# Layer 3's end in another order: the first element's normalisation and feed-forward blocks between the second one's last steps, the last addition and store in two

## The reference

```python
def _fq(x, delta, zp, n_bits):
    xi = _round_ste(x / delta) + zp
    xq = jnp.clip(xi, 0.0, 2.0 ** n_bits - 1.0)
    return (xq - zp) * delta
def _attn(x, ctx, wq, wk, wv, wo, bo, dq, dk, dv, dw):
    ...
    sim = jnp.einsum('bhid,bhjd->bhij', _fq(q, dq, 128.0, 8), _fq(k, dk, 128.0, 8)) * SCALE
    attn = jax.nn.softmax(sim, axis=-1)
    out = jnp.einsum('bhij,bhjd->bhid', _fq(attn, dw, 0.0, 8), _fq(v, dv, 128.0, 8))
    return out.transpose(0, 2, 1, 3).reshape(b, n, D) @ wo + bo
h1 = _ln(x, ln1_g, ln1_b)
x = _attn(h1, h1, a1_wq, a1_wk, a1_wv, a1_wo, a1_bo, d_q1, d_k1, d_v1, d_w1) + x
h2 = _ln(x, ln2_g, ln2_b)
x = _attn(h2, context, a2_wq, a2_wk, a2_wv, a2_wo, a2_bo, d_q2, d_k2, d_v2, d_w2) + x
h3 = _ln(x, ln3_g, ln3_b)
hg = h3 @ ff_w1 + ff_b1
a, g = jnp.split(hg, 2, axis=-1)
x = a * jax.nn.gelu(g, approximate=False) @ ff_w2 + ff_b2 + x
```

## Time and profile before

| | |
|---|---|
| runs, us | 547.52, 543.25, 539.63 (median 543.25) |
| profiled execution, us | 540.42 |
| its span, first to last instruction, us | 538.5 |
| mean granted TensorE clock | 0.784 of full |
| busy: PE, DVE, ACT, POOL | 77%, 66%, 47%, 45% |
| hidden blocks and output products of the feed-forward, from the first record to the last | 511.4 to 535.0 us |

### The profile page before, as it was taken

The page is one execution under the profiler, slowest core; times in us unless marked ns, Lnnn a source line. Parts: engine busy times, 40 slices in busy tenths (PEclk is TensorE's granted clock), DMA queues, the critical chain, the costliest instruction groups (busy, mean ns, idle before and its releaser), DMA issues.

```text
span 538.5 us, 8140 instructions
## 1 busy us (share of the span) xinstructions
PE 412.6 (77%) x2775; PEld 206.4 (38%) x2775; DVE 354.9 (66%) x802; ACT 254.0 (47%) x513; POOL 241.6 (45%) x378
## 2 busy tenths in 40 slices
PE   6889678757788999998989772566665756778597
PEld 3546455424334344334243550222232223324536
DVE  2744754556999311447384469999989898778442
ACT  2314433324000666643426327899977783447431
POOL 4051224349000344533201315999978896336320
PEclk9868957978999999999699996555555555556699
DMA  9400000000000000000000002698876677113301
GB/s 262 156 1 1 4 1 1 0 0 1 2 0 1 1 1 2 1 1 1 0 1 2 1 2 39 132 144 140 162 131 117 117 123 153 27 34 67 71 0 40
DMA packets 88975, 26.10 MB, mean 48 GB/s; under 512 B 81061, under 2 KB 88167, under 8 KB 88935
## 3 DMA queue, kind: packets, MB, share of 16 engines
q1 hardware_dynamic: 88935, 25.58, 24.5%
HBM read 5.61 MB, written 0.52 MB: 11 GB/s over the span
## 4 chain that ended last, share of the span: by engine, by line
PE 43%; DVE 27%; POOL 18%; issue 5%; ACT 4%; DMA 1%; POOLq 0%; DVEq 0%; ACTq 0%
POOL k_stack L573 12%; DVE k_stack L2068 8%; PE ps L837 5%; PE ps L852 4%; PE ps L638 3%; POOL stats L564 3%; PE ps L739 3%; DVE stats L2148 3%; PE ps L749 2%; DVE xh L1639 2%; PE ps L915 2%; DVE st L1630 2%; PE ps L630 2%; POOL rstd L483 2%; PE ps L773 2%
## 5 line engine op out<-in xcount | busy, mean ns | idle before, releaser
L2148 DVE TENSOR_REDUCE stats<-ps 128x2 f32<-128x1024 f32 x64 | 77.6, 1213 | 2.4 <-PE ps L1293 2.0
L1595 ACT ACTIVATE e_buf<-ps,stats,sders 128x512 f32<-128x512 f32 x88 | 67.6, 773 | 18.4 <-POOL stats L564 18.4
L1313 PE MATMUL ps<-k_stack,q_stack 128*32 128x128 bf16 x512 | 38.3, 307 | 37.9 <-DVE k_stack L2161 37.9
L573 POOL TENSOR_SCALAR k_stack<-e_buf,stats 128x512 int16<-128x512 f32 x88 | 63.0, 728 | 2.1 <-DVE stats L2155 1.5
L1441 ACT ACTIVATE e_buf<-ps 128x1024 f32<-128x1024 f32 (+3 forms) x44 | 28.2, 710 | 58.5 <-PE ps L837 58.5
L481 POOL TENSOR_SCALAR rstd<-mv 128x4 f32<-128x4 f32 x18 | 4.4, 243 | 99.3 <-DVE mv L1633 99.3
L1313 PEld LDWEIGHTS ps<-k_stack,q_stack 128*32 128x32 bf16 x512 | 22.0, 129 | 68.8 <-DVE k_stack L2161 66.0
L430 POOL TENSOR_SCALAR_AFFINE_SELECT e_buf<-e_buf 128x256 f32<-128x256 f32 x44 | 17.8, 412 | 66.8 <-ACT e_buf L1441 66.2
L1293 PE MATMUL ps<-q_stack 32*128 32x512 bf16 x128 | 37.6, 588 | 12.4 <-ACT e_buf L1595 8.9
L2068 DVE TENSOR_REDUCE k_stack<-ps 128x4 f32<-128x1024 f32 (+3 forms) x32 | 44.9, 1483 | 2.6 <-PE ps L796 2.6
L837 PE MATMUL ps<-k_stack,q_stack 32*128 32x512 f32 (+3 forms) x256 | 34.7, 478 | 0.6 <-ACT e_buf L1441 0.4
(11 more groups left out here) (277 smaller groups left out, 892.9 us busy)
## 6 DMA issues: line engine op xcount, KB each, us to landing
wsq<-in_squares SPq DMA_DIRECT2D x3, 384.0 KB, 4.8
k_stack<-k_stack SPq DMA_TRANSPOSE x64, 3.1
spread<-in_spread SPq DMA_DIRECT2D x1, 896.0 KB, 6.7
x<-in_x SPq DMA_DIRECT2D x1, 512.0 KB, 4.4
l_w<-in_L_xattn_W_ff SPq DMA_DIRECT2D x2, 256.0 KB, 7.2
l_w<-in_L_xattn_fc_w SPq DMA_DIRECT2D x2, 256.0 KB, 7.8
l_w<-in_L_xattn_ff_w SPq DMA_DIRECT2D x1, 512.0 KB, 8.8
out<-x SPq DMA_DIRECT2D x2, 256.0 KB, 2.3
```

The source lines that it names most:

```text
L573: pool.tensor_scalar(t_rows[n % TURNING][:, j, :], e_ring[n % len(e_ring)][:, j, :], stats[:, 2, c:c + 1], 0.0, ALU.mult, ALU.add).then_in ...
L1313: mm = pe.matmul(ps[BAND * band:BAND * (band + 1), 7, qb * P:(qb + 1) * P], v_band[:, kb, b, V * band + v, :], t_keys[n % len(t_keys)][:, ...
L1595: act.activation(e_ring[n % len(e_ring)][:, j, :], ps[:, 2 * (n % 3) + j, :], ACT.Exp, bias=stats[:, 1, c:c + 1], scale=sders[:, 8:9], acc ...
L2148: dve.tensor_reduce(stats[:, 0, c:c + 2], ps[:, 2 * (n % 3):2 * (n % 3) + 2, :], AX, ALU.max, negate=True).then_inc(S("ints.nm"), 1)
```

## The change

Five edits, all in layer 3's end.

- PE: the first element's transposes and hidden block 0 come between the outputs of tiles 6 and 7. Block 1 comes after them, then the second element's projection, blocks 2 and 3, the first element's 16 products in two parts with the second element's transposes between, blocks 4 to 7, the second element's 16 products in two parts.
- DVE: `normal` of the first element comes before `keys` of tile 6. The gating of blocks 0 and 1 comes before the second element's addition and statistics, that of 2 and 3 before its `normal`, that of block 4 before the first element's last addition.
- ACT: `cross_out(1)` comes after the gelu of block 0.
- Banks: hidden blocks use 0 to 3, which the cross attention's scores had, so block 0 also waits for the last exponentials. The first element's transposes go to bank 6, the second's to 7.
- End: the second element's last 128 x 512 addition is two of 128 x 256, from banks 5 and 6, and its 256 KB store is two of 128 KB.

```diff
@@ -98,7 +98,7 @@
 PROJECTED_AT, ADDED_AT, RSTD_AT, TURNED_AT, QUERIES_AT, CROSS_AT = 40, 40, 44, 48, 50, PAIRS + 2
-HIDDEN = (2, 3, 6, 7)
+HIDDEN = (0, 1, 2, 3)
 PV_BEHIND = 2
@@ -350,7 +350,7 @@
         states = [(name, k) for names in (("L1.sa",), ("L1.ca",), ("L1.ff",), ("L2.sa",), ("L2.ca0", "L2.ca"),
-                                          ("L2.co", "L2.ff"), ("L3.sa",), ("L3.ca0", "L3.ca"), ("L3.co",), ("L3.ff",))
+                                          ("L2.co", "L2.ff"), ("L3.sa",), ("L3.ca0", "L3.ca"), ("L3.co", "L3.ff"))
                   for k in range(B) for name in names]
         def state(name, k):
@@ -418,8 +418,14 @@
                                            flat_rows[i % len(flat_rows)]).then_inc(done, 16)
             for k in range(B):
                 sp.wait_ge(S(final), count(*final.rsplit(".", 1)) + final_each * (k + 1))
-                sp.dma_start(half_rows(out_dram, k), half_rows(x, k)).then_inc(S("out.stored"), 16)
-            sp.wait_ge(S("out.stored"), 16 * B)
+                if stop >= 3 and k == B - 1:
+                    sp.dma_start(out_dram[:, T - 2:T, :], x[:, T - 2:T, :]).then_inc(S("out.stored"), 16)
+                else:
+                    sp.dma_start(half_rows(out_dram, k), half_rows(x, k)).then_inc(S("out.stored"), 16)
+                if stop >= 3 and k == 0:
+                    sp.wait_ge(S("L3.ff.part"), 1)
+                    sp.dma_start(out_dram[:, QB:T - 2, :], x[:, QB:T - 2, :]).then_inc(S("out.stored"), 16)
+            sp.wait_ge(S("out.stored"), 16 * (B + 1 if stop >= 3 else B))
@@ -749,22 +755,26 @@
                     pe.matmul(ps[:, banks[n % 4], :], tile(w1, c), half(xT, k), start=True, stop=True
                               ).then_inc(S("ff.h"), 1)
-            def gated_feed_forward(name, w1, w2):
-                pe.wait_ge(S("ffw.loaded"), 96)
-                for n in range(B * FC):
-                    k, c = divmod(n, FC)
-                    if n == FC - 1:
-                        turn_half(xh, "L3.ln3.xh", 1)
-                    if c == 0:
-                        pe.wait_ge(S("state.T"), state(name, k))
-                    if n >= 2:
-                        pe.wait_ge(S("ff.hid"), count(name, "hid") + n - 1)
-                    pe.matmul(ps[:, HIDDEN[2 * (n % 2)], :], tile(w1, c), half(xT, k), start=True, stop=True)
-                    pe.matmul(ps[:, HIDDEN[2 * (n % 2) + 1], :], tile(w1, FC + c), half(xT, k), start=True, stop=True
-                              ).then_inc(S("ff.h"), 1)
-                for k in range(B):
-                    out_rows(name, w2, k)
+            def gated(n):
+                k, c = divmod(n, FC)
+                if n == 0:
+                    pe.wait_ge(S("cross.exp"), T)
+                if c == 0:
+                    pe.wait_ge(S("state.T"), state("L3.ff", k))
+                if n >= 2:
+                    pe.wait_ge(S("ff.hid"), count("L3.ff", "hid") + n - 1)
+                pe.matmul(ps[:, HIDDEN[2 * (n % 2)], :], tile(l3_w1, c), half(xT, k), start=True, stop=True)
+                pe.matmul(ps[:, HIDDEN[2 * (n % 2) + 1], :], tile(l3_w1, FC + c), half(xT, k), start=True, stop=True
+                          ).then_inc(S("ff.h"), 1)
+            def gated_outputs(k, tiles, bank):
+                pe.wait_ge(S("ff.hid"), count("L3.ff", "hid") + FC * (k + 1))
+                for t in tiles:
+                    for c in range(FC):
+                        mm = pe.matmul(ps[:, bank, t * P:(t + 1) * P], tile(hid[:, c, :], k * QB + t), l3_w2[:, c, :],
+                                       start=(c == 0), stop=(c == FC - 1))
+                return mm
             def project_half(name, wo, k, bank):
                 pe.wait_ge(S("state.T"), state(name, k))
@@ -1106,6 +1116,10 @@
                             subtract(i - 1)
                         if i == QB - 1:
                             turn_half(xh, "L3.ln2.xh", 1, bank=7)
+                        if i == T + FLAT_VALUES_BEHIND - 1:
+                            turn_half(xh, "L3.ln3.xh", 0, bank=6)
+                            pe.wait_ge(S("ffw.loaded"), 96)
+                            gated(0)
                         if i >= FLAT_VALUES_BEHIND:
                             outputs(i - FLAT_VALUES_BEHIND)
                         if i < T:
@@ -1338,9 +1352,17 @@
                 subtract(1)
                 project_half("L3.ca0", W["L3_xattn_a1_wo"], 1, 7)
                 rest()
-                turn_half(xh, "L3.ln3.xh", 0)
+                gated(1)
                 project_half("L3.co", W["L3_xattn_a2_wo"], 1, 5)
-                gated_feed_forward("L3.ff", l3_w1, l3_w2)
+                gated(2)
+                gated(3)
+                gated_outputs(0, (0, 1), 4)
+                turn_half(xh, "L3.ln3.xh", 1, bank=7)
+                gated_outputs(0, (2, 3), 4).then_inc(S("add.o"), 1)
+                for n in range(FC, B * FC):
+                    gated(n)
+                gated_outputs(1, (0, 1), 5).then_inc(S("L3.ff.first"), 1)
+                gated_outputs(1, (2, 3), 6).then_inc(S("add.o"), 1)
@@ -1505,7 +1527,6 @@
                     if i == T:
                         cross_out(0)
                     rounded(i - FLAT_ROUND_BEHIND)
-                cross_out(1)
             def cross_out(b):
                 act.wait_ge(S("cross.pv"), QB * (b + 1))
@@ -1600,11 +1621,13 @@
                     if n == TURNED_AT:
                         state_out("L3.ca", col("L3_xattn_ln2_g"), col("L3_xattn_ln2_b"), [0], 6)
                 cross()
-                state_out("L3.ff", col("L3_xattn_ln3_g"), col("L3_xattn_ln3_b"), [0])
+                state_out("L3.ff", col("L3_xattn_ln3_g"), col("L3_xattn_ln3_b"), [0], 6)
                 for n in range(B * FC):
                     c = n % FC
-                    if n == FC - 2:
-                        state_out("L3.ff", col("L3_xattn_ln3_g"), col("L3_xattn_ln3_b"), [1])
+                    if n == 1:
+                        cross_out(1)
+                    if n == FC:
+                        state_out("L3.ff", col("L3_xattn_ln3_g"), col("L3_xattn_ln3_b"), [1], 7)
                     act.wait_ge(S("L3.ff.h"), count("L3.ff", "h") + n + 1)
                     if n >= 2:
                         act.wait_ge(S("L3.ff.hid"), count("L3.ff", "hid") + n - 1)
@@ -1912,9 +1935,10 @@
                             add_to_x("L3.co", 6, [0])
                             stats_of("L3.co.x", 0, range(QB))
                             means_of(0)
+                        if i == T + FLAT_SUMS_BEHIND:
+                            normal("L3.ln3", 0)
                         if i >= FLAT_KEYS_BEHIND:
                             keys(i - FLAT_KEYS_BEHIND)
-                    normal("L3.ln3", 0)
                 return maxima, recips, rest
@@ -2199,16 +2223,30 @@
                         cross_maxima(1)
                 cross_recips(0)
                 rest()
-                add_to_x("L3.co", 4, [1])
-                moments("L3.ln3", 1, "L3.co.x", 1)
-                for n in range(B * FC):
+                def gate(n):
                     k, c = divmod(n, FC)
-                    if n == 1:
-                        normal("L3.ln3", 1)
                     dve.wait_ge(S("L3.ff.gel"), n + 1)
                     dve.scalar_tensor_tensor(half(hid[:, c, :], k), ps[:, HIDDEN[2 * (n % 2)], :], col("L3_xattn_ff_b1", c),
                                              gel[:, n % 2, :], ALU.add, ALU.mult).then_inc(S("L3.ff.hid"), 1)
-                add_to_x("L3.ff", 4)
+                gate(0)
+                gate(1)
+                add_to_x("L3.co", 4, [1])
+                moments("L3.ln3", 1, "L3.co.x", 1)
+                gate(2)
+                gate(3)
+                normal("L3.ln3", 1)
+                gate(4)
+                add_to_x("L3.ff", 4, [0])
+                for n in range(FC + 1, B * FC):
+                    gate(n)
+                dve.wait_ge(S("L3.ff.first"), 1)
+                dve.wait_ge(S("L3.ff.biased"), count("L3.ff", "biased") + 2)
+                dve.tensor_tensor(x[:, QB:T - 2, :], ps[:, 5, 0:2 * P].rearrange("p (t d) -> p t d", d=D),
+                                  x[:, QB:T - 2, :], ALU.add).then_inc(S("L3.ff.part"), 1)
+                dve.wait_ge(S("L3.ff.o"), count("L3.ff", "o") + B)
+                dve.tensor_tensor(x[:, T - 2:T, :], ps[:, 6, 2 * P:4 * P].rearrange("p (t d) -> p t d", d=D),
+                                  x[:, T - 2:T, :], ALU.add).then_inc(S("L3.ff.x"), 1)
 def kernel(**inputs):
```

## The result

| | before | changed |
|---|---|---|
| median, us (20 runs each) | 539.46 (537.27 to 547.92) | 543.37 (541.53 to 549.44) |
| profiled execution, its span, us | 540.42, 538.5 | 541.80, 539.9 |
| mean granted TensorE clock | 0.784 | 0.779 |

The ratio of changed to before is 1.007, with a 95% interval from 1.0047 to 1.0093; timed again (first experiment) it is 1.0045, from 1.0014 to 1.0077. The change makes the kernel slower by some 2.4 to 3.8 us, which is far under 2% but clear of the noise.

What follows compares the result with a forecast made beforehand. PE's list was taken to bound this end: +0.45 - 1.25 - 0.6 + 0.85 + 1.65 + 1.65 = +2.75 us, with the tail 2.2 slower. That gave 542.6 or 545.4 by base, forecast 544.0, range 539.5 to 549.0.

Steps and rivals of the forecast that it cites:

- Step 1: The first element's `normal` ahead of tile 6's keys: PE's ten products of tile 6 start later, +0.45 us.
- Step 2: Transposes and block 0 ahead of tile 7's outputs: PE waits about 0.85 us ahead of block 0, before 1.25.
- Steps 3 and 4: Each element's 16 output products behind its own fourth block: PE waits for that block's gating, +1.65 us each.
- Step 5: The second element's `normal`, held back by gating on DVE, still precedes PE's need by 0.7 us: costs nothing.
- Step 6: The tail, last addition and store in halves: 0.3 us saved on each, -0.6 us.
- The sum: PE's terms give +2.75 us, its last product at 537.8; with the tail the kernel is 2.2 us slower.
- Rival 1: The clock falls in PE's new waits: +5 us, 549.0, or 3% slower if it stays down; chance 0.13.
- Rival 2: The clock rises by 508.6 instead of about 513.6: 2.4 us gained, undoing the 2.2, 541.6; chance 0.12.
- Rival 3: The second element's chain comes 2 us late: PE waits 1.3 us at its transposes, 545.3; chance 0.07.
- The level: Kernel time 544.0 us, the middle between 542.6 on the profiled execution's base and 545.4 on the runs' median.
- No change that can be measured: Whole kernel: 2.2 us slower is too little, as runs spread 1.5% and a measurement can tell about 2%.
- The range: Kernel time from 539.5 to 549.0 us, with chance 0.95 of staying within 2%.

Runs made afterwards that it cites:

- first experiment: The changed kernel run again with no edit, for a second trace; ratio to before 1.0045 (1.0014 to 1.0077).
- block 0 back: The changed kernel with hidden block 0 behind tile 7's outputs again; ratio to before 1.0013 (0.9982 to 1.0045).
- filled: The changed kernel with an unread 128 x 256 fp32 product in PE's wait ahead of block 0; ratio to before 0.9991 (0.9965 to 1.0018).
- products late: The changed kernel with all 16 output products of the first element behind block 7; ratio to before 1.005 (1.0013 to 1.0088).

## Why the prediction was right, step by step

- **The bound.** PE's list sets this end: in every kernel the last chain is PE with its waits, and each edit moved the end by what it did to them and to the clock.
- **Step 1** (tile 6's outputs 0.45 us later): from tile 5's to tile 6's outputs it is now 2.76 us (502.54 to 505.30) where it was 2.40: 0.36 us. But the term is too small here. Tile 6's outputs start 2.5 us after the mark in both traces of the changed kernel and 1.45 us before, so 1.05 us later (0.4 to 1.1 over the six traces with this order). The transposing DMA of tile 6 had landed about 2.1 us before its keys in the first trace and 1.1 in the second (issued at 499.26 and 500.83, 3.4 us to landing, keys at 504.75 and 505.28), so its keys no longer waited for it but for `normal`, and `normal` for POOL's root (1.24 us idle). The sum had taken both chains as they lay in before's one trace, where the root was ready 0.7 us ahead of the landing; the sign "0.45 us later after the landing" did not come.
- **Step 2** (0.85 us ahead of block 0): 0.96. Its length was right. What the sum left out is that this wait bears on the clock: without it (block 0 back, or filled) the clock rose 2.8 to 3.9 us sooner. In the sum it made no difference, since before had its 1.25 us in the same place and rose as late (10.0 us after the mark against 9.7 and 8.7).
- **Steps 3 and 4** (1.65 us each): 1.56 and 1.56. That both are the open gelu and gating is shown by the tile whose products covered 0.9 us of the second.
- **Step 5** (costs at nothing): the cover of 0.7 us held, `normal` done at 521.52 and needed at about 522.5. How close it is, the kernel with the products late shows: without them PE waits 2.59 us for it.
- **Step 6** (tail -0.6): -0.8. The addition saved 0.27, as taken, and the store 0.51, near the row's bound of 0.45 and not the 0.3 that I took. The Trainium skill (DMA: Bandwidth & Descriptors, Anatomy of one DMA) gives 0.3 for the bytes as well, an estimate from its rate, which was fitted to DMAs that GpSimd issues, while these are SP's; the median landing of 2.3 us for 256 KB and 1.8 for 128 KB says 0.5.
- **The sum** had +2.2 us; from the mark the traces have +2.1 and +1.7. That it comes so close is in part luck, as two errors cancel. PE's last product ends 2.9 and 2.5 us later after the mark than before, against 2.75 in the sum. In this, tile 6's outputs are 1.05 us later (0.45 in the sum), PE's waits from there on 4.08 us against 1.85, so 2.2 more (2.3), and its work is 0.4 and 0.8 us shorter (0 in the sum). It is shorter because the clock rises 7.1 and 6.3 us after tile 6's outputs start, where it took 8.6 before. Timed, it is 1.007 and 1.0045, where 2.2 us are 1.004. The second interval holds the forecast, the first just misses it. What the missing 0 to 1.6 us are is open; the two traces don't show them.
- **Rival 1** (the clock falls in the new waits) did not come: full speed through both waits in each of the two traces. Its mechanism exists, as the products-late kernel shows at 523.75. The two rows of before at full speed were a good guide for waits of 1.56 us. The rule of the Trainium skill (TensorE: Matmul & The Clock Gate, Why this matters for your kernels) warns of PE-idle gaps longer than any of PE's waits behind the mark, so the prediction was wrong to set it against this change, and full speed through 1.56 us agrees with it. What it does not cover is the products-late trace, where 2.59 and 0.87 us close together were enough.
- **Rival 2** (the clock rises earlier) did not come in the changed kernel, because of the wait ahead of block 0, as was written against it. A little of it did come: from the mark the rise is 0.3 and 1.3 us sooner, still after block 0 began. It came in full as soon as that wait was gone.
- **Rival 3** did not come.
- **The level**: 544.0 was taken between two bases. The sum on the profiled execution's own base gave 542.6, that on the three runs' median 545.4; measured is 543.37. That this is so close is luck too. The middle of the bases, 541.8, is 2.4 us above the 539.46 of 20 runs, and the change of 2.2 is 1.7 below the 3.9 between the medians; with the right base the sum would have said 541.7.
- **"No change that can be measured"** was wrong: with 20 runs a side the interval begins at 1.0047, clear of 1, though the change is only a third of 2%.
- **The range**: its low end of 539.5 is not what its own terms give. The tail by its other bound saves 0.8 instead of 0.6, so 540.2 goes to 540.0. The result lies far above either.

## What to carry to other kernels

Work that is spread out to fill an early wait takes the cover from a later one: before moving a step, write down which latency the old order hid behind it. Here the output products hid the last gelu and gating; moving half of them ahead opened it twice. A move in an in-order list is best made where the moved piece's own input is ready: the transposes filled the wait for the keys, while block 0 behind them only traded it for ACT's copy.

## What the runs showed of the hardware

A product that nobody reads, in a wait of 0.96 us, took nothing and brought the clock's rise 2.8 to 3.8 us forward (8.7 and 9.7 us after the mark to 5.9), in its one trace, and a real reordering that closed the same wait did the same (5.8). A PE with two waits of 1.51 and 0.96 us and otherwise busy can stay at half speed: 7.03 of 9.50 us busy in the changed kernel at 0.50, while 21.33 of 24.50 us with two waits of 1.56 stayed at 1.00. The kernels reach the mark between 500.07 and 505.75 us, which is more than the whole change; with such a spread a change in the last 40 us is better read from a mark than from the span, and the mark's own scatter of 0.7 us has to be known.
